# Five expert tiles between the pieces of the last batch's tail, and every subtraction of the row maximum on GpSimd

## The reference, cut to what matters

```python
x = x + tanh(g_xattn) * attention(layernorm(x), ctx, ctx, adj, mask)   # softmax(QK^T/4 + adj, masked) V, Wo
h = layernorm(x)
probs = softmax(h @ gate_w.T);  e = argmax(probs)                      # one expert of 8 per token
y = relu(h @ w1[e] + b1[e]) @ w2[e] + b2[e]                            # 256 -> 1024 -> 256
x = x + tanh(g_ffn) * probs[e] * y
```

## Time and profile before

| | |
|---|---|
| median of 3 runs | 622.31 us (622.23 to 623.06) |
| the profiled execution | 623.12 us, of it 621.3 us in the span that the profile shows |
| PE busy | 528.8 us, 85% of the span |
| PE weight loads | 401.0 us, 65% |
| DVE, ACT, POOL busy | 297.5, 303.9, 308.1 us |
| mean granted TensorE clock | 0.945 |
| read from and written to HBM | 69.5 and 14.2 MB |

### The profile page before, as it was taken

How to read it: one execution, slowest core, us unless ns; L and a number is a source line. 1 busy time by engine, 2 the same in 40 slices (tenths; PEclk the granted TensorE clock), 3 DMA queues, 4 the chain that set the end, 5 groups by cost and what they waited for, 6 DMA issues and landing times.

```text
span 621.3 us, 13413 instructions
## 1 busy us (share of the span) xinstructions
PE 528.8 (85%) x4008; PEld 401.0 (65%) x4009; DVE 297.5 (48%) x883; ACT 303.9 (49%) x674; POOL 308.1 (50%) x475
## 2 busy tenths in 40 slices
PE   4579999899999899999899988510989999999992
PEld 3247566566666566666566665310989999998882
DVE  2656677776678775678566876340011111111110
ACT  3536676556685556686566755200333333333320
POOL 6443485763584663584655537122344445445341
PEclk9879999999999899999899998955899999999997
DMA  8664139612149520149400181855455655555630
GB/s 294 213 215 138 64 103 210 136 68 70 40 139 198 102 69 2 60 133 194 92 2 2 51 271 45 288 108 138 113 184 181 204 191 205 195 190 185 186 93 1
DMA packets 62649, 83.43 MB, mean 134 GB/s; under 512 B 8920, under 2 KB 52008, under 8 KB 62472
## 3 DMA queue, kind: packets, MB, share of 16 engines
q1 hardware_dynamic: 58504, 74.53, 43.2%
q0 software_dynamic: 4096, 8.29, 4.6%
HBM read 69.54 MB, written 14.18 MB: 135 GB/s over the span
## 4 chain that ended last, share of the span: by engine, by line
PE 24%; DMA 16%; issue 9%; POOL 6%; DVE 5%; ACT 2%; POOLq 1%; DVEq 0%; SPq 0%; ACTq 0%
DMA out_y<-cT,sidx 13%; PE bank L809 6%; PE bank L821 5%; PE bank L799 3%; POOL rows L623 3%; PE bank L906 2%; PE bank L896 2%; DVE prob L1218 2%; DMA slot_d<-pair,posi 2%; PE bank L702 1%; ACT pt L986 1%; PE bank L783 1%; PE bank L737 1%; DMA rows<-xn_d,gidx 1%; PE bank L764 1%
## 5 line engine op out<-in xcount | busy, mean ns | idle before, releaser
L1218 DVE CUSTOM_DVE_ANT_0 prob<-bank,adjm 128x512 f32<-128x512 f32 x256 | 172.7, 688 | 95.5 <-issue 63.0
L571 POOL TENSOR_SCALAR prob<-prob,negmax 128x512 f32<-128x512 f32 x192 | 134.3, 704 | 143.4 <-DVE negmax L1218 135.4
L986 ACT ACTIVATE pt<-bank 128x512 f32<-128x512 f32 x256 | 150.9, 595 | 100.1 <-PE bank L809 94.4
L809 PE MATMUL bank<-ident,prob 128*128 128x128 f32 x1024 | 156.7, 276 | 7.3 <-POOL prob L571 3.4
L809 PEld LDWEIGHTS bank<-ident,prob 128*128 128x128 f32 x1024 | 126.7, 142 | 47.0 <-POOL prob L571 13.4
L1051 ACT ACTIVATE adjm<-bank,colsm 128x128 f32<-128x128 f32 x184 | 52.6, 368 | 113.9 <-PE bank L896 113.9
L799 PE MATMUL bank<-w2s 128*128 128x512 bf16 x256 | 99.4, 390 | 6.2 <-DMA w2s<-part_d 5.5
L1337 DVE TENSOR_TENSOR cT<-bank,maski 128x256 f32<-128x256 f32 x23 | 9.8, 424 | 172.1 <-PE bank L906 172.1
L896 PEld LDWEIGHTS bank<-xT,pt 128*128 128x128 f32 x736 | 88.3, 197 | 2.2 <-ACT xT L1042 1.0
L896 PE MATMUL bank<-xT,pt 128*128 128x128 f32 x736 | 88.6, 280 | 0.6 <-ACT xT L1042 0.6
L906 PE MATMUL bank<-w2s,adjm 128*128 x368 | 83.4, 380 | 0.0
(11 more groups left out here) (141 smaller groups left out, 502.3 us busy)
## 6 DMA issues: line engine op xcount, KB each, us to landing
pt<-in_L_ffn_w SPq DMA_DIRECT2D x23, 1024.0 KB
w2s<-part_d SPq DMA_DIRECT2D x48, 256.0 KB
w2s<-in_L_ffn_w SPq DMA_DIRECT2D x8, 1024.0 KB, 10.6
part_d<-parts SPq DMA_DIRECT2D x16, 384.0 KB, 2.6
maski<-in_mask_Bx1xSxS_ik SPq DMA_DIRECT2D x4, 1024.0 KB, 6.2
w2s<-part_d SPq DMA_DIRECT2D x32, 128.0 KB, 3.0
xres<-in_x SPq DMA_DIRECT2D x18, 128.0 KB
x_d<-rows SPq DMA_DIRECT2D x18, 128.0 KB, 2.5
```

Of the source, the lines that this page charges most:

```text
L571: po.tensor_scalar(prob[:, m], prob[:, m], -1.0, negmax[:, m:m + 1], ALU.mult, ALU.add).then_inc(s_shpool, 1)
L809: mm = pe.transpose(tr_bank[n % NTB][:, c * P:(c + 1) * P], prob[:, n % TILES % NB, c * P:(c + 1) * P], ident[:])
L986: act.activation(pt[:, g % 2, :, j, q2 * P:(q2 + 1) * P], tr_bank[c % NTB][:].rearrange("p (c q) -> p c q", c=QT), ACT.Exp).then_inc(s_cac ...
L1218: ve.tensor_tensor_reduce(out=prob[:, m % NB], in0=sc_bank[m % NS][:], in1=adjm[:, qt], scale=-1.0, scalar=BIG, op0=ALU.add, op1=ALU.min, ...
```

## The change

Three things, in one diff.

1. `ACT_SHIFTS = ()`: all 256 subtractions of the maximum are POOL's, where 64 were ACT's.
2. In the last batch's step tables the tail of the batch before comes earlier ("rank" at step 36 where it was 51), and behind it DVE computes a first table: for the tokens of the first three batches (`KNOWN` = 1536) it finds five full tiles (`EARLY` = 5) that are certain whatever the last batch brings. w1 and w2 of the first two of them (4 MB) are loaded at once into buffers that are free by then, then the list entries; POOL gathers their rows at steps 56 to 62.
3. The expert work of these five tiles is written out between the pieces of the last tail on every engine; the first turning comes at step 66. The other 18 slots (`LATE`) run in the loop as before; the second table (over the rest) has the links of the first, and two or three instructions more. The w2 of an early tile is loaded a second time (5 MB more in all). SP's queue now has: `tail_pair` of rows 0 and 1, half of w2, b2, a wait for the first table, w1 and w2 of early tiles 0 and 1, a wait for the scatters, the five list entries, `tail_pair` of rows 2 and 3, the other half of w2, and w1 and w2 of early tiles 2 to 4 with the last rows between them, each load behind a wait for PE to be done with its buffer; only then the wait for the second table, w1 of the first two late slots, the wait for the last scatters and the late list entries.

```diff
-    ACT_SHIFTS = (3, 6)
+    ACT_SHIFTS = ()
-    LAST_USES = [u for u in USES if not u[1].startswith("next")]
+    LAST_USES = sorted([(10, "values", 0), (11, "values", 1), (13, "heads", 0), (14, "heads", 1), (16, "turn", 0),
+                        (17, "turn", 1), (19, "out", 0), (21, "out", 1), (26, "normed", 0), (27, "normed", 1),
+                        (29, "gate", (0, 1)), (36, "rank", 0), (45, "heads", 2), (46, "heads", 3), (48, "turn", 2),
+                        (49, "turn", 3), (51, "out", 2), (53, "out", 3), (58, "normed", 2), (60, "gate", (2,)),
+                        (61, "normed", 3), (63, "gate", (3,))], key=lambda use: use[0])
+    SLOT_STEPS, SCATTERED_STEP = ((53, 54, 55, 57), (38, 39, 40, 41)), (72, 55)
+    TABLE_STEPS, INDEX_STEP, GATHER_STEPS = (38, 39, 40, 41, 42, 43), 56, (57, 58, 59, 60, 61, 62)
...
 (SyncE)
+            sp.wait_ge(e_eid, 1)
+            for s in range(2):
+                early_w1(s)
+                early_w2(s)
+            sp.wait_ge(r_scat, B * (16 * QT))
+            for s in range(EARLY):
+                at = sp.value_load(base_i[0:1, s:s + 1], min_val=0, max_val=X * TOK)
+                sp.dma_start(slots[:, s], slot_d[ds(at, P), :]).then_inc(e_slots, 16)
+            tail_pair(last, last * QT, 2, last * QT + 2)
             sp.wait_ge(s_score, B * TILES)
             for e in range(X // 2, X):
                 load_w2(e)
-            tail_pair(B, NT - 2, 0, None)
+            early_w1(2)
+            early_w2(2)
+            rows_out(B, NT - 2, 0)
+            rows_out(B, NT - 2, 1)
+            early_w1(3)
+            early_w2(3)
+            rows_free(B, 0)
+            early_w1(4)
+            early_w2(4)
...
             sp.wait_ge(r_eid, 1)
+            for v in range(2):
+                load_w1(v, v)
+            sp.wait_ge(r_scat, (B + 1) * (16 * QT))
+            for v in range(2):
+                load_slots(v, v)
...
 (GpSimd)
+            def early_index():
+                wait_apart(po, e_slots, 16 * EARLY)
+                po.tensor_copy(eidx[:], slots[:, 0:EARLY, 0]).then_inc(e_idx, 1)
+                wait_apart(po, e_idx, 1)
...
                 if last:
+                    if n == INDEX_STEP:
+                        early_index()
+                    if n in GATHER_STEPS[0:EROWS]:
+                        early_normed(GATHER_STEPS.index(n))
+                    if n in GATHER_STEPS[EROWS:]:
+                        early_x(GATHER_STEPS.index(n) - EROWS)
...
             for k in range(2):
                 tail_rstd(B, k)
+            for s in range(EROWS, EARLY):
+                early_normed(s)
+            early_x(EROWS)
+            early_scatter(0)
             pairs(B)
             for t in range(QT):
                 to_slots(t)
...
 (TensorE; early_turn is 2 transposes, early_hidden half of 32 matmuls, early_y half of 16)
+            for n in range(LAG, TILES + 2):
                 step(B - 1, n, LAST_USES, True)
+            pe.wait_ge(s_masked, B * TILES)
+            early_turn(0)
+            for n in range(TILES + 2, TILES + LT):
+                step(B - 1, n, LAST_USES, True)
+            early_hidden(0, 0)
+            for c in range(QT):
+                weigh(B - 1, GROUPS - 1, c)
+            early_hidden(0, 1)
+            early_turn(1)
             pe.wait_ge(s_osb, B * GROUPS + 2)
-            for i, (n, what, k) in enumerate(TAIL_A):
-                tail_use(B, i + LAST_SHIFT, what, k)
+            last_tail("heads", 0)
+            last_tail("heads", 1)
+            early_y(0, 0)
+            last_tail("turn", 0)
+            last_tail("turn", 1)
+            early_y(0, 1)
+            last_tail("out", 0)
+            last_tail("out", 1)
+            early_hidden(1, 0)
+            early_hidden(1, 1)
+            early_turn(2)
+            last_tail("normed", 0)
+            last_tail("normed", 1)
+            early_y(1, 0)
+            last_tail("gate")
+            early_y(1, 1)
+            early_hidden(2, 0)
+            last_tail("rank")
+            early_hidden(2, 1)
+            for s in range(2, EARLY):
+                if s + 1 < EARLY:
+                    early_turn(s + 1)
+                for half in range(2):
+                    early_y(s, half)
+                if s + 1 < EARLY:
+                    for half in range(2):
+                        early_hidden(s + 1, half)
...
-            with pe.Fori(0, SLOTS // 2) as i:
-                for u in range(2):
-                    expert(i * 2 + u, i, u)
-            expert(SLOTS - 1, SLOTS // 2, 0, True)
+            with pe.Fori(0, LATE // 2 - 1) as i:
+                for v in range(2):
+                    expert(i * 2 + v, i, v)
+            expert(LATE - 2, LATE // 2 - 1, 0)
+            expert(LATE - 1, LATE // 2 - 1, 1, True)
...
 (VectorE)
+                if last:
+                    if n == TABLE_STEPS[0]:
+                        early_count()
+                    if n == TABLE_STEPS[1]:
+                        early_sum()
+                    if n == TABLE_STEPS[2]:
+                        early_experts()
+                    if n == TABLE_STEPS[3]:
+                        early_places()
+                    if n == TABLE_STEPS[4]:
+                        early_done()
```

More of the change, by code:

```diff
@@ L209, in build @@
         gidx = sb("gidx", [P, 2], I32)
+        eidx = sb("eidx", [P, EARLY], I32)
+        least, done, stepd = (sb(n, [P, X]) for n in ("least", "done", "stepd"))
         xidx = sb("xidx", [P, 2], I32)
@@ new lines, in early_y @@
+            def early_y(s, half):
+                u = s % 2
+                if half == 0:
+                    pe.wait_ge(f_tmp, s + (2 if s in (1, 2) else 1))
+                    pe.wait_ge(e_w2[u], 32 * (s // 2 + 1))
+                for c in range(half * FC // 2, (half + 1) * FC // 2):
+                    pe.wait_ge(f_hT, s * FC + c + 1)
+                    second = c >= ew2_cut[u]
+                    w = ew2[u][second][:, c - second * ew2_cut[u]]
+                    mm = pe.matmul(early_y_bank(s), hT[:, u, c], w, start=c == 0, stop=c == FC - 1)
+                if half == 1:
+                    mm.then_inc(f_y, 1)
@@ L1005, in step @@
                         next_use(b, i, what, k, b + 1)
-                if n == EXP_STEP:
+                if n == EXP_STEP[last]:
                     route_exp(b)
@@ new lines, in expert_of, with last_tail @@
+            def expert_of(s):
+                return act.value_load(eid[0:1, ds(s, 1)], min_val=0, max_val=X - 1)
+            def last_tail(what, k):
+                i = next(i for i, (n, w, a) in enumerate(TAIL_A) if w == what and a == k)
+                tail_use(B, i + LAST_SHIFT, what, k)
+            for n in range(LAG, TILES + 2):
+                step(B - 1, n, LAST_USES, True)
+            act.wait_ge(e_eid, 1)
+            turned_rows(0, 0)
+            for n in range(TILES + 2, TILES + LE):
+                step(B - 1, n, LAST_USES, True)
@@ new lines, in _, with expert @@
+            turned_rows(2, 0)
+            last_tail("normed", 0)
+            last_tail("normed", 1)
+            route_exp(B)
+            for s in range(2, EARLY):
+                e = expert_of(s)
+                for half in range(2):
+                    hidden(s, s % 2, e, half)
+                if s + 1 < EARLY:
+                    turned_rows(s + 1, (s + 1) % 2)
+            def expert(j, v, last=False):
+                u = (v + EARLY) % 2
+                e = act.value_load(eid[0:1, ds(j + EARLY, 1)], min_val=0, max_val=X - 1)
+                for half in range(2):
+                    hidden(j + EARLY, u, e, half)
@@ new lines, in last_tail @@
+            def last_tail(what, k=0):
+                i = next(i for i, (n, w, a) in enumerate(TAIL_A) if w == what and (what == "gate" or a == k))
+                tail_use(B, i + LAST_SHIFT, what, TAIL_A[i][2])
+                return i + LAST_SHIFT
+            ve.wait_ge(r_b2, 16)
+            last_tail("heads", 0)
+            last_tail("heads", 1)
+            early_out(0)
+            for k in range(2):
+                last_tail("out", k)
+                row_stats(B, k)
+            for k in range(2):
+                norm_row(B, k)
@@ L1311, in _ @@
             then(ve.tensor_reduce(tiles[:], cmp_t[:], AX.X, ALU.add))
-            then(ve.tensor_scalar(span[:], tiles[:], -float(P), float(TOK), ALU.mult, ALU.add))
+            then(ve.tensor_tensor(tiles[:], tiles[:], done[:], ALU.subtract))
+            then(ve.scalar_tensor_tensor(out=span[:], in0=tiles[:], scalar=-float(P), in1=stepd[:], op0=ALU.mult, op1=ALU.add))
             src, dst = tiles, end
```

439 lines of the change are left out of this document (287 added, 152 removed).

## The result

The change makes the kernel faster, by 1.0 to 1.5% and not by the 3.6% that was forecast. The median of four executions is 618.03 us against 622.68. One of the four, 625.41 us, was a slow one, and the ratio, 0.9897 (95% interval 0.9849 to 0.9946), leaves it out. The same kernel was timed twice more beside the experiments: 0.9851 (0.9784 to 0.9918) and 0.9871 (0.9827 to 0.9915). The time is outside the range of 587 to 608. The profiled execution took 617.65 us with a span of 615.8.

The account below looks back on a forecast made before the run. PE was taken to bound attention and loop, with waits in the tail. First late hidden blocks at 450.2 + 17 x 7.56 + 1.4 + 18.4 = 598.5 us of span against 621.3, given as 600 us, range 587 to 608.

Parts of the forecast that it names:

- The bound: PE bounds attention and loop, not the tail; the gain depends on when the first late slot's hidden blocks begin.
- path 2: DMA chain into the late loop (scatter, list entries, gather, PE): ends last, first late hidden blocks at 450.2 us.
- Start of the tail: When the attention's last transposes end: 391.0 us in the kernel before, put at 394.0 in the changed one.
- The first table: DVE in the last batch, steps 38 to 41: 17 links, 4.6 us, before `e_eid`; table's end put at 361.
- The moved pieces: Tail pieces put earlier in the last batch: step 41 at 358 with them in front, no delay given for them.
- POOL at the end: Last batch from step 56: POOL stands 4 us for entries, then 1 us gathers; 2.6 us delay, ends 0 and 9.
- The subtractions on POOL: Attention: 64 subtractions move from ACT to POOL at 704 ns each; taken as 0, between 4 us less and 4.5 more.
- rival C: POOL late at step 56 and in the subtractions: transposes end 3 to 9 us later, 603 to 609 us; chance 0.20.
- B: Rival: PE's own work, not the DMAs, sets the late loop's start; 588 us as a median, 591 with delay; chance 0.27.
- D: Rival: slower than before, POOL gates PE in the attention; 0.7 us per moved subtraction gives 644 us; chance 0.03.
- E: Rival: early tiles' loads come so late that they run behind the tail, 37 us come back, 622 us; chance 0.02.

Follow-up runs that it names:

- e6: The changed kernel with the first table's five functions at steps 38, 40, 42, 44 and 50 instead of 38 to 42; 612.63 us, 0.9862 to before.
- e10: The changed kernel with two subtractions of eight on ACT, table spread, early entries before early loads, late entries before the second late w1; 600.41 us, 0.9656 to before.
- e7: The changed kernel with the five early list entries loaded before w1 and w2 of the first two early tiles; 612.09 us, 0.9870 to before.
- e1: The kernel before with only one part of the change, all subtractions on POOL; 624.62 us against 622.29, 1.0035.
- e13: The changed kernel with two subtractions of eight back on ACT, a repeat run; 608.89 us against 613.67 for the changed kernel, 0.9793 to before.
- e3: The changed kernel with the last batch's tokens marked dead, so the four last scatters write nothing; 606.39 us, 0.9734 to before.
- e4: The kernel before with w1 of slot 0 issued only when the last scatters have landed; 620.56 us, one execution.
- e9: The changed kernel with the late list entries asked for before w1 of the first two late tiles; 609.78 us against 611.46, 0.9782 to before.

## Why the prediction was wrong

**The bound, right.** The late tiles keep their period, (597.2 - 466.6) / 17 = 7.7 us, the end is the same, the hole is filled with the early tiles' work, and path 2 ends last: the gain is set by when the first late tile can begin.

**"Start of the tail": this step failed.** I gave 3.0 us of delay (87.0 for the stretch), it is 12.2 (96.2), from terms that I costed at nothing or one by one:
- The first table. I costed its links for the path of `e_eid` (4.6 us) and never as DVE time in front of the masks. Five steps hold 24 links and 5 masks: from the mask at 357.66 to that behind the last link at 368.99 are 11.3 us, for five steps of 1.25; before, the same five took 4.3. The scores have three buffers in turn (`NS = 3`), a cover of three steps that is then used up: 4.4 us of waiting, and half clock right behind it for some 6.7 us (0.26 of 12.9, twice). e6 shows the wait itself gone, and that this gives back 1.9 us at tile 48 and not all.
- The moved pieces. The prediction put step 41 at 358 "with the earlier pieces in front of it", over 3 us later than in the kernel before, and gave them nothing in the delay of the end. They stand at 3.8 us at tile 38; how much of it is left at the end stays open. e10 has 4.1 us left there, but PE still waits 1.5 us for `negmax` and 3.4 for POOL in it.
- POOL at the end. The prediction names the gather of 1 us in each of steps 57 to 62, beside a subtraction of 0.70, and takes 2.6 us for all of it, the wait included. A step with both takes 1.9 us, so six are 4 us too long against 1.25, behind 2.5 us at the index; against the kernel before, whose steps are longer there too, the stretch from tile 56 to the end costs 3.3. e7 is worth 3.2 us in B. (The entries, put at 380.5 where the terms given add up to 379.8, reach POOL at 391.3, and step 56 is at 386.3 and not at 376.5.)
- The subtractions on POOL. "I take 0, between ends of 4 us less and 4.5 more": alone they cost 0.35% (e1), in the changed kernel some 5 us (e13), at the upper end. Nearly 2 of them are in the batches ahead of the last; the rest meets the gathers and scatters on POOL's queue in the last batch, where I had worked out each without the other. That was rival C's place, but only in part its terms (POOL stood 2.5 us before the index, not 5 and more), and its price, 606 in the middle, was too low.

**Path 2: the mechanism right, one size off.** "The scatters' 8-byte rows slow everything until they have landed" holds (e3, e4). I carried over the landing of before, 9.5 us, to a place with 4 MB of loads in flight; it is 11.9 to 15 there. That is the term that was mis-sized, by 2.4 to 5.5 us, and with it the loads: w1 of early tile 4 took 11.0 us (12.7 forecast), but that of the second late tile 20.9, and tile 4's w2 in between them kept PE waiting 6.7 us.

**The rivals.** B has nothing for it: PE idles 12.7 us between 447 and 466.6. D fell: e1 loses 2 us, not 22. The rule of the Trainium skill on the shared port pair (SBUF — State Buffer, section "SBUF: two separate sides") agrees with single instructions of the table: four of them start while a subtraction runs on POOL and take 0.55 to 0.65 us, where their like take 0.2. But with a fifth, beside a scatter's issue, they are some 2 us of the 12. E did not occur.

What stays open: what fixes the scatters' own 9 us, in which the DMA engines show no work; why it is 11.9 us in one profile and 16.3 in another; and what the moved pieces alone cost.

## What to carry to other kernels

Cost an added chain of small instructions twice: for those who wait for its result, and as time of its engine in front of the next regular work; five short functions in five steps made DVE the bound of a stage that PE had bounded. Work that moves to an earlier place makes everything behind it later, also when the sum of the work stays. When bulk loads are moved beside a latency chain, the chain's own DMAs must be costed with that traffic: put list entries and indices ahead of the bulk loads in the queue (e7: 3.2 us of the stretch), and keep scatters of tiny rows away from both. Ahead of the loads is not enough where a gather follows: in e9 the gather met the loads in the entries' place. And hidden work that engine queues share (subtractions, gathers, scatters on one engine) has to be summed step by step at the place where they meet, not as a busy share of the batch.

## What was not expected of the hardware

Four scatters of 128 rows of 8 bytes land 8.8 us behind the last one with nothing beside them (e4), with the DMA engines' share at 0.01. They take 11.9 to 16.3 us beside bulk loads, and 4.35 us beside the same loads when their rows are dropped (e3). In that time a load of 1 MB takes 11 to 21 us instead of 4.7, while the DMA engines look busy (a share of 0.85 at 101 GB/s, and 0.99 at 367 without the writes).
